# A two-layer graph network on one core: visits that begin at borders of pairs of steps, and a PE that signals by drains

## The reference, cut to what matters

```python
# N = 6250 nodes, D = 512, 106250 edges (src, dst), sorted by dst; self-loops are among them
deg  = segment_sum(ones, src, N)
dinv = where(deg > 0, rsqrt(max(deg, 1)), 0)
norm = -dinv[src] * dinv[dst]
def cheb_conv(x, W0, W1, b):
    tx1 = segment_sum(x[src] * norm[:, None], dst, N)
    return x @ W0 + tx1 @ W1 + b
h   = layer_norm(cheb_conv(x, W1_0, W1_1, b1), gamma, beta)
h   = where(h >= 0, h, 0.01 * h)
out = layernorm(x + cheb_conv(h, W2_0, W2_1, b2))
```

## Time and profile before

| | us |
|---|---|
| median of 3 runs | 2662.75 |
| lowest and highest | 2658.46, 2668.54 |
| the profiled execution's own time | 2677.57 |
| its span, first to last instruction | 2675.8 |
| PE busy | 2033.7 (76%) |
| POOL busy | 1608.5 (60%) |
| DVE busy | 978.8 (37%) |
| ACT busy | 414.5 (15%) |

### The profile page before, as it was taken

One profiled execution on the slowest core, in us unless ns is written; L12 is line 12 of the kernel. 1 busy time (PEld: TensorE's weight loads), 2 busy tenths in 40 slices (PEclk: granted clock), 3 DMA queues, 4 the chain that ended last, 5 costly groups with the idle time before them and its releaser, 6 DMA issues.

```text
span 2675.8 us, 28699 instructions
## 1 busy us (share of the span) xinstructions
PE 2033.7 (76%) x8006; PEld 970.8 (36%) x8006; DVE 978.8 (37%) x1503; ACT 414.5 (15%) x844; POOL 1608.5 (60%) x1721
## 2 busy tenths in 40 slices
PE   5258787877888887887884778777787878777887
PEld 5223333333333343443441333333333333333333
DVE  9943333332333333333332233333333333333333
ACT  4401111121222122121221000000000000000001
POOL 0466555666566666666654666666666666666663
PEclk7579888998899899999997889988898888989988
DMA  6576666666576677676756666766666676677674
GB/s 213 193 221 201 195 197 193 198 200 209 178 214 213 205 214 211 200 213 208 208 184 195 195 211 205 215 214 204 213 208 203 212 223 205 206 214 217 207 217 136
DMA packets 191838, 546.41 MB, mean 204 GB/s; under 512 B 32382, under 2 KB 32384, under 8 KB 191692
## 3 DMA queue, kind: packets, MB, share of 16 engines
q0 software_dynamic: 133120, 436.31, 55.3%
q10 hardware_dynamic: 44644, 81.69, 8.5%
q1 hardware_dynamic: 13928, 26.50, 2.7%
HBM read 493.03 MB, written 51.34 MB: 203 GB/s over the span
## 4 chain that ended last, share of the span: by engine, by line
PE 34%; another core or an unknown queue 30%; issue 17%; DVE 11%; ACT 5%; ACTq 1%; POOL 1%; DMA 1%; DVEq 0%; SPq 0%
PE bank L696 14%; PE bank L689 14%; PE bank L751 3%; DVE acc L1136 2%; DVE ring L890 2%; PE bank L638 2%; DVE onehot L1031 1%; DVE work L1012 1%; DVE stats L1067 1%; ACT feat L515 1%; ACT work L494 1%; ACT work L505 1%; DVE ring L892 1%; POOL ring L389 1%
## 5 line engine op out<-in xcount | busy, mean ns | idle before, releaser
L389 POOL DMA_INDIRECT ring<-table,index x1664 | 1574.8, 946 | 941.0 <-issue 468.3
L689 PE MATMUL bank<-ring,onehot 128*128 x4096 | 996.3, 399 | 166.1 <-issue 65.9
L1136 DVE TENSOR_TENSOR acc<-acc,bank 128x512 f32 x512 | 351.4, 686 | 1621.5 <-remote 829.6
L689 PEld LDWEIGHTS bank<-ring,onehot 128*128 128x128 f16 x4096 | 417.8, 102 | 697.8 <-issue 312.0
L696 PE MATMUL bank<-wA,work 128*128 128x512 f32 x784 | 414.8, 679 | 138.4 <-ACT work L494 115.7
L696 PE MATMUL bank<-wB,base_in 128*128 128x512 f32 x784 | 379.0, 628 | 38.2 <-DVE acc L1102 30.8
L1031 DVE TENSOR_TENSOR onehot<-bank,rel 128x1024 f16<-128x1024 f32 x256 | 311.6, 1218 | 0.1
L696 PEld LDWEIGHTS bank<-wA,work 128*128 128x128 f32 x784 | 166.6, 218 | 344.2 <-issue 204.8
L751 PE MATMUL bank<-diag,acc 128*128 128x128 f32 x784 | 135.4, 325 | 168.2 <-DVE acc L1136 98.7
L696 PEld LDWEIGHTS bank<-wB,base_in 128*128 128x128 f32 x784 | 154.5, 204 | 206.2 <-issue 165.5
L751 PEld LDWEIGHTS bank<-diag,acc 128*128 128x128 f32 x784 | 114.4, 224 | 192.8 <-DVE acc L1136 124.5
(11 more groups left out here) (121 smaller groups left out, 672.8 us busy)
## 6 DMA issues: line engine op xcount, KB each, us to landing
ring<-table,index POOLq DMA_INDIRECT x1664
feat<-in_x ACTq DMA_DIRECT2D x96, 256.0 KB
table<-work SPq DMA_DIRECT2D x49, 256.0 KB, 2.7
hidden_t<-feat ACTq DMA_DIRECT2D x49, 256.0 KB
table<-work ACTq DMA_DIRECT2D x49, 256.0 KB
base_in<-hidden_t ACTq DMA_DIRECT2D x49, 256.0 KB
out<-work ACTq DMA_DIRECT2D x48, 256.0 KB
acc<-in_x SPq DMA_DIRECT2D x6, 1792.0 KB, 18.6
```

Of the source, the lines that this page charges most:

```text
L389: nc.gpsimd.indirect_dma_start(out=ring[:, at * ROW:(at + 1) * ROW], out_offset=None, in_=table[l], in_offset=bass.IndirectOffsetOnAxis(ap ...
L689: last = nc.tensor.matmul(bank[n % SUM_BANKS][:, :], hot, ring[:, bass.ds(slot_at + (2 * j + half) * D, D)], start=j + half == 0, stop=j + ...
L1136: nc.vector.tensor_tensor(acc_at, acc_at, bank[n % SUM_BANKS][:, :], ALU.add).then_inc(sums_added, 1)
```

## The change

Places become even: 8.75 + 5.22 v, cut down to an even number, so that visits begin between two pairs of steps. FIRST_PLACE is now in 256ths of a step, and lateness computes the same places on the chip. DVE's leaky part moves to the place itself (LEAKY_LATER 0) and its statistics to two steps behind it (STATS_LATER 2). No matmul in the walk increments a semaphore any more. Behind the second step of each pair PE issues a drain, which increments steps_done by 2. A drain follows the turned sums (sums_turned). In begin, one drain follows the raw transpose and tells raw_turned, and a plain increment behind it tells normed_turned. In complete, turn_hidden is now ahead of sums_product, one drain behind both tells out_done, and a plain increment tells back_done. What stands behind the last step has a drain for each signal.

```diff
--- before.py
+++ after.py
@@ -89,8 +89,8 @@
     BIAS_PARTS = 3
 
     SPACING = STEPS * 256 // TILES
-    FIRST_PLACE = -(-STEPS // TILES) + 8 // GROUP
-    PRODUCT_LATER, LEAKY_LATER, STATS_LATER = 2, 1, 3
+    FIRST_PLACE = 35 * 64
+    PRODUCT_LATER, LEAKY_LATER, STATS_LATER = 2, 0, 2
     COLS = CHUNKS
     PAD_NODE = TILES * P - 1
     WHOLE_GROUPS = E // SPAN
@@ -98,7 +98,7 @@
     NO_NODE = 1 << 14
     assert STEPS % (2 * BLOCK) == 0 and STEPS % SUM_BANKS == 0 and GROUPS % RING == 0 and GROUPS % USED == 0
     assert STEPS % LOADED == 0
-    assert EARLY_STEP < FIRST_PLACE and STEPS == 256 and FIRST_PLACE > 0
+    assert EARLY_STEP < FIRST_PLACE >> 8 and STEPS == 256
     assert STEPS % SUM_BANKS == 0 and BOUNDS % SLOTS == 0
     assert HIST * HIST_VISITS == COLS and STEPS * GROUP <= 1024 and STEPS <= 448 and RING & (RING - 1) == 0 and GROUPS <= 512
     assert TILES == LOADS * LOAD == 49 and GROUP_BLOCKS == 2 and WHOLE_GROUPS == GROUPS - 1
@@ -281,7 +281,7 @@
 
         def place(v):
 
-            return min(STEPS, FIRST_PLACE + (v * SPACING >> 8))
+            return min(STEPS, FIRST_PLACE + v * SPACING >> 8 & -BLOCK)
 
         def visits_late(eng, early, visit, unrolled=False):
 
@@ -633,10 +633,9 @@
             nc.tensor.matmul(bank[7][:, 0:1], count[0:1, 0:P], ones_f[0:1, 0:1], start=True, stop=True
                              ).then_inc(part_done, 1)
 
-            def turn(src_tile, to, count_sem):
+            def turn(src_tile, to):
                 for c in range(KB):
-                    last = nc.tensor.transpose(to[:, c * P:(c + 1) * P], src_tile[:, c * P:(c + 1) * P], ident[:, :])
-                last.then_inc(count_sem, 1)
+                    nc.tensor.transpose(to[:, c * P:(c + 1) * P], src_tile[:, c * P:(c + 1) * P], ident[:, :])
 
             for v in range(HIST_VISITS):
                 pe.wait_ge(hot_ready, v + 1)
@@ -686,16 +685,16 @@
                         if j == GROUP - 1 and half == 1 and n + 1 < STEPS:
 
                             wait(pe, sums_added, g + 1 - SUM_BANKS + 1)
-                        last = nc.tensor.matmul(bank[n % SUM_BANKS][:, :], hot,
+                        nc.tensor.matmul(bank[n % SUM_BANKS][:, :], hot,
                                                 ring[:, bass.ds(slot_at + (2 * j + half) * D, D)],
                                                 start=j + half == 0, stop=j + half == GROUP)
-                last.then_inc(steps_done[l], 1)
+                if n % BLOCK == BLOCK - 1:
+                    nc.tensor.drain().then_inc(steps_done[l], BLOCK)
 
             def dense(to, x_of, w, start):
                 for c in range(KB):
-                    last = nc.tensor.matmul(to[:, :], x_of[:, c * P:(c + 1) * P], w[:, c * D:(c + 1) * D],
-                                            start=start and c == 0, stop=not start and c == KB - 1)
-                return last
+                    nc.tensor.matmul(to[:, :], x_of[:, c * P:(c + 1) * P], w[:, c * D:(c + 1) * D],
+                                     start=start and c == 0, stop=not start and c == KB - 1)
 
             def turn_normed(v):
 
@@ -703,7 +702,7 @@
                 pe.wait_ge(normed_ready, k + 1)
                 pe.wait_ge(sums_moved, v if v < TILES - 1 else TILES)
                 wait(pe, hidden_moved, k)
-                turn(normed[k % 2], bank[TURN_BANK], normed_turned)
+                turn(normed[k % 2], bank[TURN_BANK])
 
             def turn_hidden(v):
 
@@ -711,14 +710,14 @@
                 pe.wait_ge(hidden_ready, k + 1)
                 wait(pe, split1_done, k)
                 pe.wait_ge(raw_moved, min(v + 2, TILES))
-                turn(feat[:, k % 2, :], bank[BACK_BANK], back_done)
+                turn(feat[:, k % 2, :], bank[BACK_BANK])
 
             def turn_raw(k):
 
                 pe.wait_ge(s_raw[k % 2], 16 * (k // 2 + 1))
                 wait(pe, split1_done, k - 2)
                 wait(pe, raw_moved, k)
-                turn(feat[:, 2 + k % 2, :], bank[BACK_BANK], raw_turned)
+                turn(feat[:, 2 + k % 2, :], bank[BACK_BANK])
 
             def base_product(l, v):
 
@@ -748,30 +747,37 @@
                     wait(pe, hidden_moved, min(v, TILES - 2))
                 wait(pe, sums_moved, TILES * l + v)
                 for c in range(KB):
-                    last = nc.tensor.matmul(bank[TURN_BANK][:, c * P:(c + 1) * P],
+                    nc.tensor.matmul(bank[TURN_BANK][:, c * P:(c + 1) * P],
                                             acc[:, bass.ds(v * D + c * P, P)], diag[:, v % 2, :],
                                             start=True, stop=True)
-                last.then_inc(sums_turned, 1)
+                nc.tensor.drain().then_inc(sums_turned, 1)
 
             def sums_product(l, v):
 
                 pe.wait_ge(sums_moved, TILES * l + v + 1)
-                dense(out_bank(numbered(v)), sums_t[v % 2], wA, False).then_inc(out_done, 1)
+                dense(out_bank(numbered(v)), sums_t[v % 2], wA, False)
 
             def begin(l, v, steps):
                 if l == 0 and v > 0:
                     turn_normed(v)
                 if l == 0 and v == 0:
                     turn_raw(0)
+                    nc.tensor.drain().then_inc(raw_turned, 1)
                 if l == 0 and v + 1 < TILES:
                     turn_raw(v + 1)
+                    nc.tensor.drain().then_inc(raw_turned, 1)
+                    if v > 0:
+                        pe.sem_inc(normed_turned, 1)
                 base_product(l, v)
                 turn_sums(l, v, steps)
 
             def complete(l, v):
-                sums_product(l, v)
                 if l == 0 and v > 0:
                     turn_hidden(v)
+                sums_product(l, v)
+                nc.tensor.drain().then_inc(out_done, 1)
+                if l == 0 and v > 0:
+                    pe.sem_inc(back_done, 1)
 
             def both(l):
                 def visit(it):
@@ -809,11 +815,16 @@
                 turn_sums(l, v, STEPS)
                 if l == 0:
                     turn_normed(v)
+                    nc.tensor.drain().then_inc(normed_turned, 1)
                 sums_product(l, v)
+                nc.tensor.drain().then_inc(out_done, 1)
                 if l == 0:
                     turn_hidden(v)
+                    nc.tensor.drain().then_inc(back_done, 1)
                     turn_normed(v + 1)
+                    nc.tensor.drain().then_inc(normed_turned, 1)
                     turn_hidden(v + 1)
+                    nc.tensor.drain().then_inc(back_done, 1)
 
         @block.vector
         def _(dve):
@@ -903,11 +914,11 @@
 
             def lateness():
 
-                assert all(place(v) == FIRST_PLACE + (v * SPACING >> 8) for v in range(BOUNDS)) and place(BOUNDS) == STEPS
-                link(nc.vector.tensor_scalar(place_i[:, 0:1], part_i[:, :], SPACING, None, ALU.mult))
+                assert all(place(v) == (FIRST_PLACE + v * SPACING >> 8 & -BLOCK) for v in range(BOUNDS)) and place(BOUNDS) == STEPS
+                link(nc.vector.tensor_scalar(place_i[:, 0:1], part_i[:, :], SPACING, FIRST_PLACE, ALU.mult, ALU.add))
                 link(nc.vector.tensor_scalar(place_i[:, 1:2], place_i[:, 0:1], 8, None, ALU.arith_shift_right))
-                link(nc.vector.tensor_copy(place_f[:, 0:1], place_i[:, 1:2]))
-                link(nc.vector.tensor_scalar(place_f[:, 1:2], place_f[:, 0:1], float(FIRST_PLACE), None, ALU.add))
+                link(nc.vector.tensor_scalar(place_i[:, 0:1], place_i[:, 1:2], -BLOCK, None, ALU.bitwise_and))
+                link(nc.vector.tensor_copy(place_f[:, 1:2], place_i[:, 0:1]))
                 link(nc.vector.tensor_tensor(late[0:BOUNDS, 0:1], bound_f[0:BOUNDS, 1:2], place_f[0:BOUNDS, 1:2],
                                              ALU.is_ge))
                 link(nc.vector.tensor_scalar(bound_f[0:BOUNDS, 2:3], part[0:BOUNDS, :], -1.0, float(TILES),
```

## The result

The changed kernel takes 2887.43 us (median of 4 runs, 2884.93 to 2904.54), the kernel before 2663.05 beside it (4 runs, 2658.46 to 2668.54). The ratio is 1.087, 95% interval 1.084 to 1.089: 8.7% slower, where 6.5% faster was forecast. The profiled execution took 2886.69 us, its span is 2884.9.

What follows compares the result with a forecast made beforehand. No engine was full; late news of PE's matmuls was taken to leave PE idle 523 us in two walks. 2677.57 - 523 + 298 + 130 - 80 = 2502.6, by the median told as 2490 us; 8 in 10: 2360 to 2800.

Steps and rivals of the forecast that it cites:

- What the drain gives back: Prediction's part on PE's 523 us idle time in the walks: a drain tells at once, so late news goes.
- The news of a drain is not carried by a matmul: Reason given why PE's drains would tell promptly in the walks, where matmuls' increments come late.
- the bunching: Two steps' adds on DVE ran one right behind the other, though PE's steps were 1.73 us apart.
- idle time of before goes: PE's idle time in the two walks, 254.2 and 268.9 us, together 523 us, goes as far as late news.
- drains and what they expose: On PE: 505 drains, 202 us, plus register loads 76 us and branches and jumps 20 us, together 298 us.
- what is late next: Idle time left to PE in both walks, from POOL's pace, the normalised tile and onehots: 130 us.
- the clock: PE's clock, granted 0.91 and 0.89, improves as long stops go: 80 us gained, ends 0 and 196.
- One drain: Cost on PE: 0.16 us lost overlap, 0.04 drain end, 0.19 restart, taken as 0.40 us.
- POOL's floor: 832 gathers a layer, one every 1.25 us, take POOL 1040 us; PE's predicted walks were 1153 a layer.
- Rivals B and C: B: POOL bounds the walks, 2320 us, chance 0.12; C: PE's new waits for DVE eat the gain, 2666, chance 0.09.
- Rival A: PE's drains bring news no sooner, or hold PE too: about 2960 us or more, chance 0.24.
- decision point of 0.75 us a drain: Cost each of PE's 505 drains may reach before all gain is gone, 0.35 more than taken.

## Why the prediction was wrong

**The step that failed** is "I take it that a drain tells at once in the walks too." (What the drain gives back). It rested on the drain behind the last product, with no gather in flight, carried over to walks in which POOL gathers all the time. In its place the trace has 428 us held. "The news of a drain is not carried by a matmul" was argued from the bunching and falls with it: the drain itself ends only when the completion is reported, and that comes late. The Trainium skill, "Perfetto Trace Analysis", section Sequencer-only Instruction, has DRAIN execute in the sequencer. The trace agrees with the place; but that execution lasts until the matmuls are reported, 9.42 us in the drain shown, of which its own matmuls still ran for 2.9.

**The sum in its terms,** us:

| term | predicted | measured |
|---|---|---|
| idle time of before goes | -523 | -523 (no wait of DVE or ACT in the walks is remote) |
| drains and what they expose | +298 | +277 (restart 244, busy time 33, the clock in it) |
| held drains | 0 | +428 |
| what is late next | +130 | +15 |
| the clock | -80 | not parted from the busy time |
| around the walks | 0 | +12 |
| in all | -175 | +209 |

The 209 are between the profiled executions, 2677.57 and 2886.69. By the medians it is 224, because that of before was 15 us slow, as the forecast had allowed for.

*One drain.* 0.40 us and what it exposes, 298/505 = 0.59 us together, was near: 277/505 = 0.55 here, with what the clock gave back taken off, and 323/505 = 0.64 without any hold. Its end, 0.04 us behind the matmul, is 0.02 where it isn't held.

*What is late next.* 130 us were too many. With PE standing at its drains, the onehots, the normalised tile and the order inside a visit were ready in time. POOL's floor wasn't reached: it waited 647 us for SP. Rivals B and C got no trial, as PE never came close.

*The clock.* Granted a little higher, but PE's busy time rose by 33 us. At full clock the same change raised it by 81 (SP filling the ring, with and without drains), so by this estimate some 48 of the 80 us did come, and the 505 drains cost 244 + 81 = 325 us, 0.64 each. Where the stops really went it was 1.00, and the first walk's busy time 913 instead of 1007.

*Rival A* came true in its first form, "it waits for what holds the tell, and PE with it". I gave it 0.24, and weighed for it the fact that decided: late only where gathers run. Its decision point of 0.75 us a drain was right in kind: the held time alone adds 428/505 = 0.85. Its price, 2960 us and more, was 70 too high: 2663 + 298 keeps all 523 us of old idle time, where the held drains and the rest come to 428 + 15. From a step's end to its add it is 2.8 us in the mean now, 3.9 before and 5.1 with the same pairs told by matmuls: the news is a little less late, but PE stands for it.

*What stays open.* Shown: with POOL issuing long rows of gathers, PE's completions are reported late, to other engines and to its own drain, in 88 of 144 cases until 1.5 to 2.0 us after the last; without POOL's gathers, never, at up to 301 GB/s; and the operands, weight form and bias that were tried make no difference. Not shown: by which part of the chip, and whether the count of gathers decides or the time that they take, which go together at 1.25 us each. Nor was a gather form tried in which POOL issues more rows at once. Of other engines' completions the trace of before shows none held: all its remote waits are waits for PE, and of the semaphore updates on record in and after its first walk 777 of DVE's come within 0.06 us of an instruction's end and 11 later, 328 and 9 of ACT's, but 242 and 473 of PE's. Many updates have no record there, so this is no full count. Also argued only: that no way of spacing the breaks can bring much here. The numbers for it are 1664 gathers of 1.25 us, 2080 us, beside 2663 - 2080 = 583 us for all else and all breaks.

## What to carry to other kernels

Don't count on a drain where the matmul's own tell is late: it ends late too, and stops the engine meanwhile. Before exchanging one tell for another, look for a row in which the new one runs under the conditions in which the old one is late. Where a semaphore moves long after the work, look at what third engine is issuing at that time, and take that away first; here SP's plain transfers in place of POOL's gathers took 25% off the time, though they can't choose rows by source. Not all of that is late news: without gathers PE's two walks take 945 + 846 = 1791 us, less than POOL's 2080.

## What the runs showed of the hardware

POOL's issuing of indirect DMAs holds back news of PE's finished matmuls: 428 us over 505 drains, single ones up to 9.3 us. It comes with long unbroken rows of gathers (in the changed kernel up to 5: no drain; 7 and 8: all the pairs' within the row, at 1.25 us each; other traces have some at fewer) and not with their bytes (436 or 55 MB). It ends 1.5 to 2.0 us after the row in 88 of 144 cases. Gaps of 0.81 and 1.39 us leave DVE 968.6 and 747.5 us of late news; gaps of 1.97 us clear it after every sixth gather (3.1 us), in part after every eighth (160.5), not after every twelfth (878.9).

An unheld drain ends 0.02 us behind the last matmul. From a drain's end to the next matmul it is about 0.5 us in the mean (244 us over the 493 drains in the walks); with the lost overlap, pairs and new places the change costs 323/505 = 0.64 us a drain where nothing is held.

The same ring filled by SP's queue took 269 and 301 GB/s in the two walks, by POOL's gathers 203 and 209.
